# Attention of a decoder layer: scaled scores written to SBUF by the row maximum, exponentials in place there, and part of the row sums taken by VectorE

## The reference

```python
q = (x @ Wq).reshape(B, T, H, Dh)          # B=4, T=512, H=16, Dh=32
scores = jnp.einsum('bthd,bshd->bhts', q, k)
mask = jnp.tril(jnp.ones((T, T), dtype=scores.dtype))
scores = scores * mask                     # masked scores are 0, not -inf
attn = jax.nn.softmax(scores / T ** 0.5, axis=-1)
out = jnp.einsum('bhts,bshd->bthd', attn, v).reshape(B, T, H * Dh)
return out @ Wo
```

## Time and profile before

| | us |
|---|---|
| median of 3 runs | 1476.02 (1475.46 to 1476.39) |
| the profiled execution | 1477.08 |
| its span, first to last instruction | 1475.4 |
| PE busy in the span | 1421.8 (96%) |
| DVE, ACT, POOL busy | 990.7, 713.2, 387.3 |
| attention of the four batches, from the first to the last exponential | 67.4 to 521.9, in four stretches of about 58 |

### The profile page before, as it was taken

One profiled execution on the slowest core, in us unless ns is written; L12 is line 12 of the kernel. 1 busy time (PEld: TensorE's weight loads), 2 busy tenths in 40 slices (PEclk: granted clock), 3 DMA queues, 4 the chain that ended last, 5 costly groups with the idle time before them and its releaser, 6 DMA issues.

```text
span 1475.4 us, 26841 instructions
## 1 busy us (share of the span) xinstructions
PE 1421.8 (96%) x8896; PEld 719.6 (49%) x8896; DVE 990.7 (67%) x2125; ACT 713.2 (48%) x1648; POOL 387.3 (26%) x703
## 2 busy tenths in 40 slices
PE   6989998998999999999999999999999999999999
PEld 4465456556645654344444444444444444444444
DVE  7786688668658867886566666665655756665533
ACT  5795279339716945344354353353343443533532
POOL 0053225204374436521221212112112211212100
PEclk9999999999999999999999999999999999999999
DMA  7554522352465521000100001001001001000011
GB/s 249 135 167 125 162 80 81 100 159 84 123 179 152 187 77 46 17 28 21 33 14 19 17 17 33 17 17 35 17 17 32 17 17 33 17 17 1 0 58 57
DMA packets 77309, 98.01 MB, mean 66 GB/s; under 512 B 8048, under 2 KB 60784, under 8 KB 76784
## 3 DMA queue, kind: packets, MB, share of 16 engines
q1 hardware_dynamic: 77168, 96.23, 21.3%
HBM read 68.94 MB, written 27.26 MB: 65 GB/s over the span
## 4 chain that ended last, share of the span: by engine, by line
PE 84%; issue 5%; DVE 4%; ACT 3%; POOL 3%; DMA 0%; ACTq 0%; POOLq 0%; DVEq 0%; SPq 0%
PE bank L887 25%; PE bank L889 24%; PE bank L888 24%; PE bank L951 2%; PE bank L972 2%; ACT prob L1268 2%; POOL nmx L766 1%; PE bank L940 1%; PE bank L900 1%; PE bank L1012 1%; PE bank L1027 1%; POOL pk L759 1%; PE bank L981 1%; PE bank L1022 1%; DVE xt L1591 1%
## 5 line engine op out<-in xcount | busy, mean ns | idle before, releaser
L887 PE MATMUL bank<-xs,G 128*128 128x512 f16 x896 | 339.8, 379 | 2.0 <-DVE c L1736 0.9
L888 PE MATMUL bank<-xs,G 128*128 128x512 f16 x896 | 339.6, 379 | 0.0
L889 PE MATMUL bank<-xs,G 128*128 128x512 f16 x896 | 339.6, 379 | 0.0
L1354 ACT COPY c<-bank 128x512 f32<-128x512 f32 x192 | 111.4, 580 | 220.2 <-PE bank L889 215.4
L1736 DVE TENSOR_TENSOR c<-bank,c 128x512 f32<-128x512 f32 x128 | 88.1, 689 | 193.2 <-PE bank L889 193.2
L887 PE MATMUL bank<-Wd,hid 128*128 128x512 f16 x512 | 194.1, 379 | 2.8 <-DVE X L1790 2.8
L889 PE MATMUL bank<-Wd,hid 128*128 128x512 f16 x512 | 194.0, 379 | 0.0
L888 PE MATMUL bank<-Wd,hid 128*128 128x512 f16 x512 | 194.0, 379 | 0.0
L751 POOL TENSOR_TENSOR c<-c,m 128x512 f32<-128x512 f32 x64 | 82.4, 1287 | 388.7 <-ACT c L1354 388.7
L1790 DVE SCALAR_TENSOR_TENSOR X<-bank,col,X 128x512 f32<-128x512 f32 x128 | 95.3, 749 | 101.6 <-PE bank L889 101.4
L1606 DVE CUSTOM_DVE_ANT_0 bank<-bank,mask,col 128x128 f32<-128x128 f32 (+3 forms) x256 | 138.9, 547 | 22.7 <-issue 18.4
(11 more groups left out here) (193 smaller groups left out, 2401.1 us busy)
## 6 DMA issues: line engine op xcount, KB each, us to landing
stack<-qk_dram SPq DMA_DIRECT2D x128, 128.0 KB, 3.4
sc_in<-scale_t SPq DMA_DIRECT2D x30, 384.0 KB
qk_dram<-qk SPq DMA_DIRECT2D x32, 256.0 KB, 2.9
packed_t<-pk_t SPq DMA_DIRECT2D x32, 192.0 KB, 1.9
pk_in<-packed_t SPq DMA_DIRECT2D x30, 192.0 KB
X<-in_x_dram SPq DMA_DIRECT2D x4, 1024.0 KB, 5.9
pk_in<-L_ffn_gate_W_packed_dram SPq DMA_DIRECT2D x16, 256.0 KB, 2.8
pk_in<-n_L_ffn_up_W_packed_dram SPq DMA_DIRECT2D x16, 256.0 KB, 3.1
```

The lines of the kernel that those rows point to most:

```text
L887: pe.matmul(o, lhs(0), rhs(0), start=first, stop=False, skip_group_check=onto)
L888: pe.matmul(o, lhs(0), rhs(1), start=False, stop=False, skip_group_check=onto)
L889: return pe.matmul(o, lhs(1), rhs(0), start=False, stop=stop, skip_group_check=onto)
L1354: nc.scalar.copy(dst[:], bank[BANK_Y if which == M5 else x][:]).then_inc(c_copied, 1)
```

## The change

1. `row_max` writes the scaled and masked scores to `prob[:, u % 2, j]` in SBUF instead of back into the bank. It takes over the waits that guard `prob`: `t_full` of tile (u-2, j), `att_full` before unit 1, and at a batch's first unit the stores that still read `prob` (`first_stored`, `sums_stored`). ACT's `exp` loses them.
2. `exp` works in place in `prob`, so it reads SBUF where it read PSUM.
3. `scores(u, j)` waits for `max_done` of the tile ahead in its bank, no longer for `exp_done`.
4. In units 1, 4, 5, 8, 9, 12 and 13 the exponentials of j = 0 and 1 no longer accumulate their sum. A new step on DVE, `first_sums`, sums both tiles with one tensor_reduce over 2 x 128 or 2 x 256 columns. It stands behind `turned(u-1, 3)`, and `all_tokens(u)` waits for it.

```diff
@@ scores (PE)
                 if u > 0:
-                    pe.wait_ge(exp_done, n * ROWS + 4 * (u - 1) + j + 1)
+                    pe.wait_ge(max_done, n * ROWS + 4 * (u - 1) + j + 1)
@@ exp (ACT)
                 act.wait_ge(shift_done, n * ROWS + 4 * u + j + 1)
-                if u >= 2:
-                    act.wait_ge(t_full, n * ROWS + 4 * (u - 2) + j + 1)
-                nc.scalar.activation(prob[:, u % 2, j, 0:wide[i]], bank[j][:, 0:wide[i]], ACT.Exp,
-                                     bias=nmx[:, u % 2, j:j + 1], accum_out=den[:, u % 2, j:j + 1]).then_inc(exp_done, 1)
+                nc.scalar.activation(prob[:, u % 2, j, 0:wide[i]], prob[:, u % 2, j, 0:wide[i]], ACT.Exp, bias=nmx[:, u % 2, j:j + 1],
+                                     accum_out=None if summed_apart(u, j) else den[:, u % 2, j:j + 1]).then_inc(exp_done, 1)
@@ row_max (DVE)
                 if u >= 2:
                     dve.wait_ge(shift_done, n * ROWS + 4 * (u - 2) + j + 1)
+                    dve.wait_ge(t_full, n * ROWS + 4 * (u - 2) + j + 1)
+                elif u == 1 and j == 0:
+                    dve.wait_ge(att_full, n * KT + KT)
                 alone(dve, s_full, n * ROWS + 4 * u + j + 1)
-                nc.vector.tensor_tensor_reduce(out=bank[j][:, 0:wide[i]], in0=bank[j][:, 0:wide[i]],
+                nc.vector.tensor_tensor_reduce(out=prob[:, u % 2, j, 0:wide[i]], in0=bank[j][:, 0:wide[i]],
@@ new (DVE)
+            def first_sums(n, u):
+                dve.wait_ge(exp_done, n * ROWS + 4 * u + 2)
+                if u >= 2:
+                    dve.wait_ge(rcol_done, n * UNITS + u - 1)
+                nc.vector.tensor_reduce(den[:, u % 2, 0:2], prob[:, u % 2, 0:2, 0:wide[u % TT]], AX.X, ALU.add).then_inc(sum_done, 1)
@@ between (DVE; the same waits leave ACT's between)
                     value_sum_out(n + 1, 2)
+                    if n == B - 2:
+                        dve.wait_ge(sums_stored, 16 * 8)
+                    elif n >= 0:
+                        dve.wait_ge(first_stored, 16 * (3, 7)[n])
                     row_max(n + 1, 0, 0)
@@ body (DVE)
                         if j == AT_TURNED and u > 0:
                             turned(n, u - 1, 3)
+                        if j == 3 and summed_apart(u, 0):
+                            first_sums(n, u)
```

More of the change, by code:

```diff
@@ L255, in decoder_layer @@
         pt_act, pt_dve, av_done, o_done, o_hi, o_lo = (sem(n) for n in ("pt_act", "pt_dve", "av_done", "o_done", "o_hi", "o_lo"))
-        den_done, rcol_done, r_full, rden_out = (sem(n) for n in ("den_done", "rcol_done", "r_full", "rden_out"))
+        sum_done, den_done, rcol_done, r_full, rden_out = (sem(n) for n in ("sum_done", "den_done", "rcol_done", "r_full", "rden_out"))
         wo_full, x1_done, mix_full, x2_done = (sem(n) for n in ("wo_full", "x1_done", "mix_full", "x2_done"))
@@ L294, in vector_copies, with summed_apart, sums_apart @@
             return 4 * (n * UNITS + u + 1) - act_copies(n, u)
+        def summed_apart(u, j):
+            return u > 0 and u % TT < 2 and j < 2
+        def sums_apart(n, u):
+            return sum(summed_apart(v, 0) for v in range(UNITS)) * n + sum(summed_apart(v, 0) for v in range(u + 1))
         def pack_slot(r, half):
@@ L1453, in between @@
                     context_heads(n + 1, (0, 1))
-                    if n == B - 2:
-                        act.wait_ge(sums_stored, 16 * 8)
-                    elif n >= 0:
-                        act.wait_ge(first_stored, 16 * (3, 7)[n])
                     exp(n + 1, 0, 0)
@@ L1494, in body @@
                     for j in range(4):
-                        if u == 1 and j == 0:
-                            act.wait_ge(att_full, n * KT + KT)
                         if u > 0:
@@ L1622, in all_tokens @@
                     dve.wait_ge(exp_done, n * ROWS + 4 * u + 4)
+                    if summed_apart(u, 0):
+                        dve.wait_ge(sum_done, sums_apart(n, u))
                     dve.wait_ge(e_zero_done, beyond_units(n, u))
```

## The result

The changed kernel takes 1479.73 us (median, 1478.67 to 1480.82); the kernel before, run beside it on the same chip, takes 1476.16 (1475.34 to 1476.76). The ratio is 1.0023, with a 95% interval from 1.0016 to 1.0031: 3.6 us slower, between 2.4 and 4.6. That is just over the 0.2% from which I called it slower, and the lower end of the interval lies under it. I had given "slower" a chance of 0.34, and 0.50 to "the same". The forecast was +2.5 us, 1478.5; the range held the time. The profiled execution's span grew from 1475.4 to 1478.2 us, by 2.8.

A forecast was written before the change was run, and what follows sets the result against it. ACT was taken to bound units 1 to 3, and a chain of waits through POOL and DVE's late divide the later groups. Terms -0.4 + 1.1 + 0.4 + 0.6 + 0.8 = +2.5 us on 1476.0 gave 1478.5 us, range 1472.5 to 1483.0.

The forecast's parts named there:

- The third wait: DVE's row maximum gets a third wait, costing 0.05 us at 3 late divides a batch: +0.6 us.
- Exponentials from SBUF: ACT's exponentials cost 0.035 us more each: +1.1 us in units 2 and 3, +0.4 us in later groups.
- Unit 1's stall: DVE's sum in unit 1 delays the row maximum of (2, 0), making exp(2, 0) 0.20 us late: +0.8 us.
- Scores released: At the end of units 1 to 3, PE's transposes start 0.10 us sooner, once a batch: -0.4 us.
- The rival in which each of the 39 waits is won: Released scores help wherever PE waits for an exponential: 39 x 0.10 = 3.9 us gained, 1472.1; chance 0.20.
- The sums from unit 4 on: DVE's sums in units 4, 5, 8, 9, 12 and 13 are hidden behind PE's values, at no cost.
- The third rival: DVE's sum doesn't fit before the first row maximum of units 6, 10 and 14: 1483.1 us; chance 0.15.
- sums without cover: If PE's values no longer hid DVE's later sums, they would cost 6.3 us beside unit 1's.
- Row maxima into SBUF: DVE's row maximum takes as long with an SBUF target as with PSUM: 0, within 0.01 us either way.
- The store waits moved to DVE: The stores of prob land before DVE's first row maximum of a batch, so nothing is added: 0.
- the signs that I had named: Trace marks: slower 512-column exponentials, scores before exp(3, 3) ends, shorter DVE waits; groups under 15.2 us would refute.

The follow-up runs named there:

- e4: Changed kernel without the row maximum's wait for t_full of the tile two units back: 1477.2 us, ratio 1.0007 to the kernel before.
- e6: Kernel before with only the row maximum's wait for t_full of the tile two units back added: 1479.0 us, ratio 1.0019.
- e7: Kernel before with exponentials reading a constant SBUF tile (the mask) instead of the scores' bank, so computing other numbers: 1479.2 us, ratio 1.0018.
- e5: Changed kernel with all its waits, but t_full and att_full in instructions of their own ahead of the wait for the scores: 1478.6 us, ratio 1.0015.
- e3: Changed kernel with unit 1's sums back in the exponentials' accumulators, the other sums kept on DVE: 1480.0 us, ratio 1.0024.
- e1: Changed kernel with the scores waiting for the exponentials (exp_done) again: 1480.8 us, ratio 1.0032.
- e12: e4 with the scores waiting for the exponentials again: 1477.6 us, ratio 1.0011.
- e2: Changed kernel with all sums back in the exponentials' accumulators, none on DVE: 1479.2 us, ratio 1.0022.
- e8: Kernel before with out_tail ahead of the third weight conversion on POOL in units 6, 10 and 14: 1473.4 us, ratio 0.9980.

## Why it came out as it did

The forecast of "a little slower" was right, and its total nearly so: 2.5 against 2.8 in the span and 3.6 in the medians (2.4 to 4.6). The terms were not. Two costs were too small and one too large, one gain was too small and one was missing, and the errors nearly cancelled: that the total came out close is in good part luck. Step by step:

**The third wait, forecast +0.6, measured +2.4 (e4) and +2.7 (e6), 2.0 in the pieces of e4.** This is the step that failed. I wrote that it is "hidden where DVE is ahead of its work, not right behind an instruction that has itself just been waited for", and took 0.05 us for the late divides only. That place was sized right: 0.29 - 0.23 = 0.06. What I passed over is the row maximum that is itself waiting for PE's scores. I had its rows: "0.71 us before unit 10" and the like the earlier trace rows. A wait that ends there doesn't hide the waits behind it. It costs 0.12 us at that place, once on the path in each of the later groups of the first three batches. With 0.06 that is 0.18 a group, and e4 and e6 measure 0.18 and 0.20.

**Exponentials from SBUF, forecast 1.1 + 0.4 at 0.035 each, measured 0.043 of pitch and +2.8 alone (e7).** The mechanism was right, the size small. I took the difference of the durations of a pair of GELU rows, and durations don't carry all of it. In the later groups I counted one exponential of unit 4, 8 or 12 at a cost and set three of unit 11 against the released scores. e7 has 0.13 a middle piece, which is three pitches of 0.043, and the release gives back only 0.07 of it. In the first piece e7 has exp(2, 0) 0.17 later (four pitches, unit 1's), exp(3, 3) another 0.30 later, and from there to the scores of unit 5 0.10 less, 2.79 against 2.89; 0.37 together.

The Trainium skill's figure ("VectorE: DVE Perf Modes", section "The TRN2 errata — SBUF-src ops pay a fixed extra latency per instruction"; 224 against 172 cycles at 1.2 GHz, an estimate of 43 ns) is what the pitch shows, and I had set it aside for the trace's number. The Trainium skill's page "Perfetto Trace Analysis", section "DVE / Act Engine Instruction (TENSOR_ADD, Activation, etc)", says that the profile's start is when an instruction begins to execute and not when it begins to fetch its data. By that rule a fetch that takes longer would lengthen the distance between starts more than a duration, and these rows agree, though no run here shows the fetch itself.

**Unit 1's stall, forecast +0.8, measured about +0.4.** DVE's row maximum of (2, 0) is as late as forecast: behind a sum of 0.68 with a pitch of 0.59. exp(2, 0) is late as well, by 0.68 us in the trace, of which 0.57 is the batch's later start. So 0.11 is its own, where I had 0.20. POOL's shift does release it, as forecast, and leaves ACT no idle time that the profile would show:

```profile
207.00 0.19 POOL L774 TENSOR_TENSOR nmx<-zero,mx 128x1 f32<-128x1 f32 x1 [1.14 <-ACT e_zero L1283]
```

It ends at 207.19 and exp(2, 0) starts at 207.22. From the row maximum's start (206.30) to the exponential's it takes 0.92 where I had 1.04, half of it because the shift comes 0.06 sooner. Even the 0.11 is not the sum's own: in e5, where the step before unit 1 is short, 0.02 is left. It comes from the third wait ahead of unit 1's first row maximum, a place where I had priced the wait at nothing, and the sum only passes it on. That the accumulators saved are "eaten by the stall" was wrong: e3 puts both back and is 0.07 a batch slower than the changed kernel.

The first piece closes with these numbers: 0.11 to exp(2, 0), 0.31 from there to exp(3, 3), and 0.18 less from exp(3, 3) to the scores of unit 5 (2.71 against 2.89, of which 0.07 is the release by e1, and 0.10 is in e7 too) make 0.24, against 19.37 - 19.14 = 0.23.

**Scores released, forecast -0.4, measured -0.07 a piece.** I expected 0.10 once a batch. It comes in the first and in both middle pieces, in e1 and in e12, and not in the last, which makes about -0.8 (12 x 0.07). The rival in which each of the 39 waits is won is refuted: the waits moved to the transposes (21.6 and 20.5 us).

**The sums from unit 4 on, forecast hidden: right** (e2). The third rival, that the sum doesn't fit, is refuted by the pitch of 0.59 and by the 0.26 us still idle before unit 10. (The price that I named for sums without cover, 6.3 us, doesn't follow from its terms: 12 x 0.60 + 12 x 0.34 is 11.3. Nothing hung on it.)

**Row maxima into SBUF, forecast 0, measured as a gain.** The duration and the pitch are as forecast: 738 ns in the mean for 512 columns against 746, and a pitch in unit 11 of 0.75 in both. What I left out is what hangs behind. From the start of a row maximum to the start of its shift, where POOL waits for it, it is 0.06 us less at every width. All nine kernels that write the row maximum to SBUF have this, and none of the five that write it to PSUM.

**The store waits moved to DVE, forecast 0: nothing shows against it either.** Who ended DVE's idle time before its row maxima is PE or POOL, never a DMA. From the groups by line and form, changed kernel:

```profile
L1609 DVE CUSTOM_DVE_ANT_0 prob<-bank,mask,col 128x256 f32<-128x256 f32 x64 | 30.0, 473 | 9.6 <-PE bank L948 8.9 <-PE bank L959 0.7
L1609 DVE CUSTOM_DVE_ANT_0 prob<-bank,mask,col 128x128 f32<-128x128 f32 x64 | 21.3, 342 | 2.4 <-POOL nmx L774 2.4
```

**Do the measured terms add up?** For a middle piece the parts measured one at a time give 15.19 + 0.13 (source, e7) + 0.18 (third wait, e4) - 0.07 (release, e1) = 15.43, and the changed kernel shows 15.31. 0.12 is missing, and e12 shows that it isn't the release. e12 is e7 with the maxima written to SBUF, the sums on DVE and one wait less ahead of the exponentials, and its piece is 15.20 against 15.32: the missing 0.12. The two traces show where it goes. These are the late row maximum of unit 11 and its shift, in e7

```profile
241.61 0.76 DVE L1606 CUSTOM_DVE_ANT_0 bank<-bank,mask,col 128x512 f32<-128x512 f32 x1
242.51 0.19 POOL L766 TENSOR_TENSOR nmx<-zero,mx 128x1 f32<-128x1 f32 x1 [1.07 <-DVE mx L1606]
```

and in e12:

```profile
240.08 0.75 DVE L1608 CUSTOM_DVE_ANT_0 prob<-bank,mask,col 128x512 f32<-128x512 f32 x1
240.92 0.19 POOL L774 TENSOR_TENSOR nmx<-zero,mx 128x1 f32<-128x1 f32 x1 [1.01 <-DVE mx L1608]
```

The shift follows after 0.84 us instead of 0.90. Counted from the scores of unit 9, this row maximum also starts 0.05 sooner (9.33 against 9.38), as is the `divide` ahead of it (9.11 against 9.15), which hangs on POOL's chain of shifts. Together the exponential behind it is 0.10 us sooner, and so is the end of the piece. e2 has the 0.12 as well and has no sums apart, so neither the sums nor the accumulator reads saved are needed for it. The target was never changed by itself, so this account rests on the traces and not on an experiment of its own.

Of the signs that I had named, the scores at the end of unit 3 do come before exp(3, 3) ends, DVE waits less before unit 5 (0.69 us, where it was 0.90), and the middle pieces stay above 15.2. The mean of 731 ns for an exponential of 512 columns tells nothing, since it was 731 before.

What the prediction said of the bound held. The path of the later groups runs through POOL and the late `divide`, and the one edit made there (e8, 3.0 us) moved as much as the largest part of the change.

## What to carry to other kernels

Count the waits of an instruction that stands at the point where two engines hand over. In these runs a wait that is long satisfied was free as long as it shared an instruction with one that blocks, but not when it made another one, either behind the wait that blocks or behind a neighbour's. Removing a wait from one instruction gains only what the next instruction on the same engine doesn't wait for as well: read both rows together. And compare pitches, not durations, when a source moves between PSUM and SBUF. When a target moves, look at the start of the instruction that waits for the result.

## What the runs showed of the hardware

- On DVE, a second instruction of semaphore waits, all satisfied, costs 0.12 us behind a wait that has just been released (step 0.18 and 0.30; e4 to e6), and 0.06 behind a `divide` that was held itself (pitch 0.23 before, 0.29 with the third wait; 0.35 in e5, where both instructions of waits also count up a semaphore).
- An exponential on ACT from SBUF has a pitch 0.043 us longer than from PSUM, in a stretch with 384 and 512 columns, though the mean durations of the two kernels for these widths are equal within 2 ns.
- The sum of two rows of 256 columns in SBUF takes 676 ns on DVE, about what one row of 512 from PSUM takes (689 ns).
- Where the row maximum wrote its main result to SBUF instead of PSUM, the instruction that reads the maximum out took 82 ns instead of 141, and POOL's shift started 0.06 us sooner (0.57 against 0.63 us after the row maximum of (1, 0)).
